# ScalarE instead of GpSimd copies each chunk's columns of tokens, with the first column loaded as an unsigned 16-bit value

## What is computed

```
x = x + attention(layernorm(x), ctx)                 # 77 context rows per batch
h = layernorm(x)
shared = (silu(h @ sg) * (h @ su)) @ sd              # 256 -> 512 -> 256, all tokens
e = argmax(h @ gate_w)                               # one of 32 experts
xs = h * sigmoid(max(h @ gate_w))
routed = (silu(xs @ rg[e]) * (xs @ ru[e])) @ rd[e]   # 1.5 MB of weights for each expert
out = x + shared + routed
```

## Time and profile before

| what | value |
|---|---|
| runs of the kernel, us | 300.6, 301.97, 305.56 (median 301.97) |
| the profiled execution, us | 302.95, with a span of 301.0 from first to last instruction |
| busy: PE, PE's weight loads | 255.7 us (85%), 181.5 us (60%) |
| busy: DVE, ACT, POOL | 154.7 us (51%), 94.2 us (31%), 88.5 us (29%) |
| granted TensorE clock, mean | 0.98 |
| transfers over the span | 68.69 MB, 228 GB/s in the mean |
| chain that ended last, by engine | PE 66%, DVE 9%, DMA 7%, issue 7%, POOL 5%, ACT 4% |
| chain that ended last, by line | L1022 25%, L947 14%, L1044 12% |

### The profile page before, as it was taken

The page is one execution under the profiler, slowest core; times in us unless marked ns, Lnnn a source line. Parts: engine busy times, 40 slices in busy tenths (PEclk is TensorE's granted clock), DMA queues, the critical chain, the costliest instruction groups (busy, mean ns, idle before and its releaser), DMA issues.

```text
span 301.0 us, 13003 instructions
## 1 busy us (share of the span) xinstructions
PE 255.7 (85%) x4627; PEld 181.5 (60%) x4629; DVE 154.7 (51%) x490; ACT 94.2 (31%) x284; POOL 88.5 (29%) x248
## 2 busy tenths in 40 slices
PE   4977899998798999979797999899899899799710
PEld 3745656653383468747676787777787677553600
DVE  0538867884399341135454555555455455433423
ACT  2048766533121011433232333333233333212000
POOL 1245211111007766012122222222222222102772
PEclk9999999999799999999999999999999999999995
DMA  6999994000001234406989499999999999924565
GB/s 197 340 371 373 375 371 174 0 3 2 0 0 71 105 107 139 139 2 217 337 288 306 154 349 315 346 382 382 375 375 383 382 374 374 316 56 106 166 210 164
DMA packets 53040, 68.69 MB, mean 228 GB/s; under 512 B 3967, under 2 KB 35100, under 8 KB 53020
## 3 DMA queue, kind: packets, MB, share of 16 engines
q1 hardware_dynamic: 46203, 61.60, 59.1%
q0 software_dynamic: 1536, 4.20, 4.5%
q10 hardware_dynamic: 5280, 2.62, 3.4%
HBM read 59.49 MB, written 8.91 MB: 227 GB/s over the span
## 4 chain that ended last, share of the span: by engine, by line
PE 66%; DVE 9%; DMA 7%; issue 7%; POOL 5%; ACT 4%; POOLq 1%; ACTq 1%; SPq 0%; DVEq 0%
PE bank L1022 25%; PE bank L947 14%; PE bank L1044 12%; PE bank L959 5%; POOL xs_flat L463 4%; DMA ring_gu<-n_L_ffn_routed_up_w_dram 3%; PE bank L878 3%; DMA slot_rows<-late 2%; DVE h_place L531 1%; PE bank L913 1%; DVE h_place L532 1%; ACT h_place L746 1%; DMA h_place<-in_L_xattn_kernel_q_dram 1%; DMA xs_flat<-slot_rows,slot_i 1%; PE bank L896 1%
## 5 line engine op out<-in xcount | busy, mean ns | idle before, releaser
L1022 PE MATMUL bank<-ring_gu,x_c 128*32 128x128 f32 x2528 | 89.9, 276 | 9.7 <-issue 6.1
L1022 PEld LDWEIGHTS bank<-ring_gu,x_c 128*32 128x32 f32 x2528 | 64.0, 109 | 28.0 <-issue 15.7
L1044 PE MATMUL bank<-ring_d,h_place 128*32 128x128 f32 x1264 | 50.5, 274 | 3.9 <-issue 0.8
L644 DVE TENSOR_TENSOR h_place<-h_place,bank 128x128 f32<-128x128 f32 x79 | 22.7, 288 | 48.8 <-ACT h_place L781 48.8
L456 POOL COPY x_c<-xs_flat 128x32 f32 x79 | 16.7, 212 | 97.2 <-PE bank L1022 84.7
L1044 PEld LDWEIGHTS bank<-ring_d,h_place 128*32 128x32 f32 x1264 | 35.1, 109 | 11.5 <-issue 10.6
L781 ACT ACTIVATE h_place<-bank 128x128 f32<-128x128 f32 x79 | 21.9, 278 | 46.4 <-PE bank L1022 45.3
L786 ACT COPY late<-bank 128x128 f32 (+1 forms) x79 | 21.0, 266 | 45.3 <-PE bank L1044 45.3
L648 DVE STREAM_TRANSPOSE h_place<-h_place 128x128 f32<-128x128 f32 x79 | 24.6, 312 | 13.5 <-PE bank L1044 8.3
L959 PE MATMUL bank<-shd,h_place 128*128 128x256 f32 x128 | 28.4, 380 | 2.1 <-DVE h_place L532 2.1
L531 DVE SCALAR_TENSOR_TENSOR h_place<-h_place,bank 128x512 f32<-128x512 f32 x16 | 11.0, 686 | 34.0 <-ACT h_place L746 34.0
(11 more groups left out here) (132 smaller groups left out, 251.2 us busy)
## 6 DMA issues: line engine op xcount, KB each, us to landing
ring_gu<-L_ffn_routed_gate_w_dram SPq DMA_DIRECT2D x32, 512.0 KB, 8.9
ring_gu<-n_L_ffn_routed_up_w_dram SPq DMA_DIRECT2D x32, 512.0 KB, 10.1
ring_d<-L_ffn_routed_down_w_dram SPq DMA_DIRECT2D x32, 512.0 KB, 10.2
slot_rows<-late ACTq DMA_DIRECT2D x10, 256.0 KB, 5.9
x<-in_x_dram SPq DMA_DIRECT2D x4, 512.0 KB, 7.0
slot_rows<-zeros SPq DMA_DIRECT2D x1, 2048.0 KB, 14.3
late<-sorted_rows SPq DMA_DIRECT2D x8, 256.0 KB, 3.2
out_dram<-x SPq DMA_DIRECT2D x8, 256.0 KB, 2.4
```

Of the source, the lines that this page charges most:

```text
L644: v.tensor_tensor(h_r, g_silu, bank[1][:, 0:P], ALU.mult).then_inc(h_ready, 1)
L1022: ins = te.matmul(bank[g][q * LW:(q + 1) * LW, 0:P].rearrange("p (m f) -> p m f", f=LW), x_c[:, k], columns[:, q], start=(k == 0), stop=(k ...
L1044: ins = te.matmul(bank[2][r:r + LW, 0:DH], hT[:, f * LW:(f + 1) * LW], ring_d[:, s, f, a * DH:(a + 1) * DH], start=(m == 0), stop=(m == HA ...
```

## The change

The table `begin` is unsigned 16-bit instead of int32. GpSimd's loop goes; what stays of it are the clearing of `late`, which now raises the semaphore `late_clear`, and the read of the number of blocks. ScalarE has a new function `take_x(c, k)`, one copy of half k, and a new function `chunk(c)`: it reads the column of chunk c+1 into a register (with no check of the value's bounds), copies half 0 of chunk c+1, does the silu of chunk c, copies half 1 of chunk c+1, and takes y of chunk c-1. Ahead of the first chunk it waits for the table, the tokens and `late_clear`, and copies both halves of chunk 0, which begins at column 0.

```diff
--- before.py
+++ after.py
@@ -10,6 +10,7 @@
 BF16 = mybir.dt.bfloat16
 I32 = mybir.dt.int32
 U32 = mybir.dt.uint32
+U16 = mybir.dt.uint16
 P = 128
 
 
@@ -186,7 +187,7 @@
         slot_i = sb("slot_i", [P, NT], I32)
         done_before = sb("done_before", [P, NE])
         begin_f = sb("begin_f", [P, 1])
-        begin = sb("begin", [1, P], I32)
+        begin = sb("begin", [1, P], U16)
         turn_first = sb("turn_first", [1, NE], I32)
         turn_end = sb("turn_end", [1, NE], I32)
         block_n = sb("block_n", [1, 1], I32)
@@ -268,6 +269,7 @@
         x0_part = sem("x0_part")
         x0_used = sem("x0_used")
         begin_ready = sem("begin_ready")
+        late_clear = sem("late_clear")
         y_taken = sem("y_taken")
         g_done = sem("g_done")
         u_done = sem("u_done")
@@ -445,18 +447,8 @@
 
 
             pool.wait_ge(table_ready, 3)
-            g_.memset(never_early, 0.0)
-            pool.wait_ge(begin_ready, 1)
-            pool.wait_ge(xsT_ready, NU + 1)
-            n_chunks = chunk_count(pool)
+            g_.memset(never_early, 0.0).then_inc(late_clear, 1)
             blocks = block_count(pool)
-            with pool.Fori(0, n_chunks) as c:
-                col = pool.value_load(begin[0:1, bass.ds(c, 1)], min_val=0, max_val=T)
-                pool.wait_ge(x0_used, c + FREE1)
-                g_.tensor_copy(x_c[:, 0], xsT[:, 0, bass.ds(col, LW)]).then_inc(x0_part, 1)
-                pool.wait_ge(u_done, c + FREE1)
-                g_.tensor_copy(x_c[:, 1], xsT[:, 1, bass.ds(col, LW)]).then_inc(x1_part, 1)
-
             pool.wait_ge(y_stored, HALVES * 16 * (blocks + 1))
             pool.sem_inc(pool_waited, 1)
             for i in range(NT):
@@ -785,6 +777,24 @@
                 act.wait_ge(down_done, c + 1)
                 a_.copy(y_halves[:, bass.ds(c, 1)].rearrange("p c d -> p (c d)"), bank[2][:, 0:DH]).then_inc(y_taken, 1)
 
+            def take_x(c, k):
+
+                act.wait_ge((x0_used, u_done)[k], c + FREE1)
+                tokens = xsT[:, k, bass.ds(col_of[0], LW)]
+                a_.copy(x_c[:, k], tokens).then_inc((x0_part, x1_part)[k], 1)
+
+            col_of = [None]
+
+            def chunk(c, first=False):
+
+                col_of[0] = nc.values_load(begin[0:1, bass.ds(c + 1, 1)], engines=(mybir.EngineType.Activation,), min_val=0, max_val=T,
+                                           skip_runtime_bounds_check_because="held to the number of tokens where it is written")
+                take_x(c + 1, 0)
+                silu(c)
+                take_x(c + 1, 1)
+                if not first:
+                    take_y(c - 1)
+
             def store_y(b, a):
                 act.dma_start(slot_c[bass.ds(STORE * b, STORE), a].rearrange("c t d -> t c d"),
                               y_all[a * LW:(a + 1) * LW, bass.ds(STORE * b, STORE)]).then_inc(y_stored, 16)
@@ -794,21 +804,23 @@
             blocks = block_count(act)
             shared_tanh(3 * KF)
             act.wait_ge(zeros_out, 16)
+            act.wait_ge(begin_ready, 1)
+            act.wait_ge(xsT_ready, NU + 1)
+            act.wait_ge(late_clear, 1)
+            col_of[0] = 0
+            take_x(0, 0)
+            take_x(0, 1)
             for j in range(STORE):
-                silu(j)
-                if j:
-                    take_y(j - 1)
+                chunk(j, first=(j == 0))
             with act.Fori(1, blocks) as b:
                 for j in range(STORE):
-                    silu(STORE * b + j)
-                    take_y(STORE * b + j - 1)
+                    chunk(STORE * b + j)
                     if j == 3:
                         act.wait_ge(y_ready, STORE * b)
                     if j in (3, 8):
                         store_y(b - 1, j // 8)
             with act.Fori(STORE * blocks, n_chunks) as c:
-                silu(c)
-                take_y(c - 1)
+                chunk(c)
             take_y(n_chunks - 1)
             act.wait_ge(y_ready, STORE * blocks)
             for a in range(HALVES):
```

## The result

The changed kernel takes 307.41 us (median of four runs, 305.8 to 309.17) against 301.67 us for the kernel before: a ratio of 1.0197, with a 95% interval from 1.0152 to 1.0243. In a second series, five rounds, the ratio was 1.010 (1.0037 to 1.0163). So it is slower, by 1 to 2%. The profiled execution took 306.83 us, with a span of 304.9 us.

A forecast was written before the change was run, and what follows sets the result against it. PE and the weight transfers were taken to run neck and neck, with steady chunks set by the silu-VectorE cycle. 3.6 + 2.5 + 1.6 + 0.9 - 0.4 - 1.7 = +6.5 us on the median 301.97 gave 308.5, range 302.5 to 316.

The forecast's parts named there:

- The cycle, +3.6 us: Steady chunks: ScalarE's read and half-0 copy before the silu make 40 chunks 0.09 us longer each; bounds 0 to 13.
- Together 0.80 against 0.71: From take_y to silu on ScalarE: index, read, copy and dispatch need 0.80 us against today's 0.71, so 0.09 late.
- `x0_used` ... does not bind: Half-0 copy's other gate, the semaphore `x0_used`, comes one part ahead of `g_done` and was claimed not to delay it.
- Rival 2: Hidden after all, not slower: silu keeps its 0.71 us, start and half the stores are absorbed; about 302.7 us, chance 0.16.
- The stores, +2.5 us: Six stores of y in the later blocks, queued on ScalarE before read and copy, delay the silu; bounds 0 to 3.6.
- 6 x 0.4: Sizing of the store term: six stores of y in the loop at 0.4 us each, giving +2.5 us.
- The place credited with -0.4: PE's one 0.28 us wait for GpSimd's copy, at 170.41 after a long register read, goes; 0.4 us gained, bounds 0 and 0.8.
- The last 15 chunks, +1.6 us: One-chunk loop at the end: the branch now precedes ScalarE's read, costing 8 chunks 0.2 us each; bounds 0 and 3.
- The start, +0.9 us: Loop start: chunk 0's copies stand behind ScalarE's shared tanh, so PE begins at 131.9, not 130.96; bounds 0.6, 1.3.
- Given back, -1.7: Near the end: a later PE waits less for weights, shrinking waits of 1.06 and 0.63 us; bounds 0 and -2.5.
- Rival 3: Copies in full in the cycle: the silu starts only when the copy has ended; 311.3 to 314 us, chance 0.11.
- Rival 4: Read not the short one: check stays or 16-bit read needs more instructions; 79 x 0.12 = 9.5 us more, 318, chance 0.12.

The follow-up runs named there:

- two_copies: Changed kernel with each half-0 copy done twice on ScalarE, the first into a spare tile nobody reads; ratio 1.0373 to the kernel before.
- int32_read: Changed kernel with the table `begin` left int32, bounds still unchecked; no total given, the read takes 279 ns and steady chunks stay at 1.45 us.
- checked_read: Changed kernel with the column read as in the kernel before, int32 and with the check of its bounds; ratio 1.028 to the kernel before.
- x_first: Changed kernel with ScalarE's copies for chunk 0 placed ahead of the shared tanh; 305.62 us, ratio 1.0101 to the kernel before.
- shift_48: Changed kernel with 48 one-column copies into a spare tile while ScalarE waits for the sorted tokens, moving its later code; ratio 1.0108 to the kernel before.

## Why the prediction was right, point by point

The forecast was 308.5 us, slower by about 2%, and 307.41 was measured. But the sum was right only as a sum, and by luck: two terms missed by 3.6 and by nearly 4 us, in opposite directions, and a gain of 1 us at chunk 10 had no term. With the second series' ratio the loss is 3 us, half of the 6.5.

- **The cycle, +3.6 us: it measured 0.** The failed step is "Together 0.80 against 0.71". On ScalarE the parts were: index 0.085 (forecast 0.1), read 0.262 (0.29), from its end to the copy 0.225 (0.25), from the copy to the silu 0.136 (0.16); together 0.708. But two waits for PE are in this: where a store makes the copy late (chunks 25, 36, 41, 52, 57), it starts 0.187 behind the end of the read, and the silu 0.124 behind the copy. So the chain by itself takes 0.66 us and has 0.05 to spare against the 0.71 that PE sets. Each part was taken from GpSimd's rows and was too long. "`x0_used` ... does not bind" was wrong as well: in steady chunks the copy waits for it some 0.04 us, which costs nothing. Rival 2's deciding point, a copy within 0.55 us, was missed by 0.02. The edge is near, though. Behind `x0_used` only 0.01 us is free, and the second copy's 0.12 lengthens each steady chunk by 0.10 (two_copies). Behind the y copy 0.05 us is free, so the 32-bit read's 0.015 is hidden (int32_read), and the check's 0.23 lengthens every second chunk by 0.20 (checked_read).
- **The stores, +2.5 us: about 6** in this profile, some 4.7 in the second one of the same kernel. The five ordinary ones behave as priced (chunk 25: +0.51, 36: +0.52, 41: +0.53, 52: +0.52, 57: +0.49), and part of it is given back in the next chunk (0.24 at 42, 0.36 at 58), which leaves about 2. The first one I sized like the others, and it cost 3.2 at once and 4.3 with what followed up to chunk 26 (4.8 less the 0.5 of chunk 25's store); in the second profile 3.0 and 2.7. The step that failed is "6 x 0.4". In the six runs in which the packet of code came during the issue or up to 0.6 us ahead of it, the issue took 1.1 to 3.0 us; in the six in which it came 1.2 us or more ahead, or not at all, 0.40 or 0.41. In all of the first six the issue ended 1.60 to 1.75 us behind the start of the packet, whenever it had begun. So its length was set by when it began, as if it waited for the fetch: it took 3.04 us in the changed kernel, where it began 1.4 us before the packet, and 1.37 in x_first, where it began 0.2 us behind it. That is why the loss at chunk 20 differs so much among kernels that are alike there. That the fetch is the cause is supported by shift_48, whose edit moved it and nothing else there, and by two_copies and checked_read, where it had moved as well; what takes up the 1.6 us, of which the packet itself is 0.31, is not shown.
- **What followed it** I had not priced at all: the fall of the clock (32 products in 1.93 and 1.27 us, not 1.08 to 1.18, some 0.8 us), which the second profile didn't have, and slow reads, 0.88 us at 169.6 and 1.10 at 179.2 against a median of 0.264, that now stand in front of the silu. The place credited with -0.4 is chunk 22, 1.79 us before the change, and 1.44 in the second profile: there the credit is right. In the first profile the lower clock covers it, and the slow reads themselves go on, on ScalarE.
- **The last 15 chunks, +1.6 us: 0.6** from chunk 64 to 74. There the copy of half 0 follows the y copy by 0.77 us (0.57 in the blocks), so the branch costs 0.2 as charged, but the single periods differ from those before by only -0.17 to +0.18.
- **The start, +0.9 us: 0.89.** **Given back, -1.7: -1.23** (chunks 75 to 78, where PE waited for weights). In the profile after, no wait of the products for weights is left, as forecast. But the second profile of the kernel before is shorter by 0.88 us in the same chunks, so at most a part of the 1.23 is shown to be the change's.
- **The two rules of the Trainium skill.** A copy from SBUF took 218 ns in the median. The Trainium skill, VectorE: DVE Perf Modes, section "The TRN2 errata", gives 213 by its figures (an estimate, 224 + 32 cycles at 1.2 GHz): this case agrees on the length. It doesn't agree that the latency stands between instructions: two copies start 0.12 us apart. The Trainium skill, DMA: Bandwidth & Descriptors, section "Latency and other measured facts", has a floor of about 600 ns for a tensor_load; the medians here are 264 to 290 ns.

Rival 3 fell with the profile after (the silu starts 0.14 us behind the start of a copy of 0.22 us) and with two_copies. Rival 2, the steady chunk unchanged, was right on the cycle and wrong on the total, since it had the stores half absorbed. Rival 4 was right in its size for the check, 0.10 per chunk (I had 0.12), and the check was absent.

## What to carry to other kernels

Before work is put in front of an instruction on the critical cycle, add up its sequencer's instructions from rows of that engine, and ask what else ever stands in that queue: here the steady chunk had room for the read by 0.05 us and for the copy by 0.01, and most of the loss came from the few chunks in which a store's issue was in the queue as well. An engine off the cycle hides rare long events (a 1 us read, a 3 us issue, a fetch of code); moved onto the cycle, each of them is paid in full. Whether such a stall also costs PE its clock differed between two executions of the same kernel (3.10 us idle, then 0.60; 2.92 us idle, then 1.00).

## What the runs showed of the hardware

- The first store of the loop took ScalarE 1.1 to 3.0 us to issue when an 8 KB packet of its code came during the issue or up to 0.6 us ahead, and 0.40 us otherwise. The long ones ended 1.60 to 1.75 us behind the packet's start. Such a packet isn't the only way to a long issue: of the four stores issued one behind the other after the loop, one took 1.05 to 1.34 us and another 0.85 to 1.03 in every kernel, with no packet of ScalarE's code near.
- For some 2 us after the first two stores of y, single reads of a register from SBUF took 0.35 to 1.10 us, on ScalarE, GpSimd and SyncE alike. Behind ScalarE's later stores they mostly kept 0.26 to 0.34, behind those from GpSimd's queue single ones took 0.41 to 1.15 again.
- On ScalarE, a silu started 0.023 us after the semaphore that it waited for, a copy whose address comes from a register 0.106 us after it (steady chunks).
- A 16-bit element was read 15 ns faster than a 32-bit one on both ScalarE (264 against 279 ns) and GpSimd (275 against 290).
